# Closing and opening steps of neighbouring attention halves in turn, with values in the keys' PSUM bank

## What is computed

```python
x = x + tanh(g_xattn[l]) * attention_l(layernorm(x), ctx, ...)   # attention half, A
x = x + tanh(g_ffn[l])   * feed_forward_l(layernorm(x), ...)     # feed-forward half, F
# layers 0, 1, 2: 16 heads of width 8 over 77 keys; layer 1 also computes a temperature per head from
# statistics of the scores; layer 3: one softmax over relu projections
# F0: two matmuls around a relu, in 8 chunks of 128 hidden units
# F1: 4 experts of 512, gated (silu(up) * gate), top 2; F2: 8 experts of 352, the same; F3: 8 experts of 128x128
```

## Time and profile before

| | |
|---|---|
| median of 3 runs | 1136.41 us (1135.51 to 1141.63) |
| the profiled execution: device time | 1137.24 us |
| its span (first to last instruction) | 1135.5 us |
| busy: PE, DVE, ACT, POOL | 83%, 63%, 40%, 9% of the span |
| mean granted TensorE clock | 0.912 of full speed |
| loading and turning of weights, before the first unit | about 66 us |
| attention units 0 to 11 | 66 to 891 us |

### The profile page before, as it was taken

One profiled execution on the slowest core, in us unless ns is written; L12 is line 12 of the kernel. 1 busy time (PEld: TensorE's weight loads), 2 busy tenths in 40 slices (PEclk: granted clock), 3 DMA queues, 4 the chain that ended last, 5 costly groups with the idle time before them and its releaser, 6 DMA issues.

```text
span 1135.5 us, 14471 instructions
## 1 busy us (share of the span) xinstructions
PE 944.7 (83%) x4795; PEld 624.7 (55%) x4795; DVE 711.9 (63%) x2190; ACT 459.6 (40%) x1101; POOL 105.9 (9%) x175
## 2 busy tenths in 40 slices
PE   2468899887777886987899899999999888979967
PEld 1434444433333355656567667666767666657744
DVE  0871433517538369579585665776776578887845
ACT  1515345455647645645635316335325222212110
POOL 3100000002103013012000100100100100000000
PEclk8669789999678898998999989999999899999987
DMA  9300000000000000000000000000000000000000
GB/s 262 118 1 1 1 1 1 1 1 1 0 1 1 1 1 1 1 1 1 1 1 2 1 1 1 1 1 1 1 1 1 1 1 10 1 10 1 1 10 9
DMA packets 12065, 12.72 MB, mean 11 GB/s; under 512 B 3758, under 2 KB 7896, under 8 KB 11992
## 3 DMA queue, kind: packets, MB, share of 16 engines
q10 hardware_dynamic: 5536, 8.04, 2.4%
q1 hardware_dynamic: 6072, 3.24, 1.1%
q0 software_dynamic: 384, 0.53, 0.3%
HBM read 10.75 MB, written 1.05 MB: 10 GB/s over the span
## 4 chain that ended last, share of the span: by engine, by line
PE 53%; DVE 28%; ACT 6%; issue 5%; POOL 2%; POOLq 0%; ACTq 0%; DVEq 0%
PE bank L1597 9%; PE bank L1585 5%; PE bank L1507 5%; PE bank L1587 4%; PE bank L1586 4%; PE bank L1392 4%; PE bank L1522 4%; DVE x L1302 3%; DVE hb L1286 3%; DVE nm L1142 3%; DVE hb L1277 3%; DVE x L1266 2%; PE bank L1562 2%; ACT PTs L946 2%; PE bank L1568 2%
## 5 line engine op out<-in xcount | busy, mean ns | idle before, releaser
L983 ACT ACTIVATE hb<-bank 96x512 f32<-96x512 f32 (+1 forms) x160 | 95.5, 597 | 262.6 <-PE bank L1587 261.7
L1585 PE MATMUL bank<-parts,m_w_lo 128*96 128x512 f32 (+1 forms) x320 | 151.0, 472 | 37.0 <-DVE hb L1277 30.0
L1597 PEld LDWEIGHTS bank<-m_w,hb 128*128 128x128 f32 (+1 forms) x1280 | 166.2, 197 | 26.8 <-issue 11.9
L1597 PE MATMUL bank<-m_w,hb 128*128 128x128 f32 (+1 forms) x1280 | 178.8, 284 | 0.5
L1286 DVE SCALAR_TENSOR_TENSOR hb<-hb,bank 96x512 f32<-96x512 f32 (+1 forms) x160 | 108.9, 680 | 87.8 <-ACT hb L983 87.4
L1587 PE MATMUL bank<-parts,m_w_hi 128*96 128x512 f32 (+1 forms) x320 | 128.9, 403 | 0.0
L1586 PE MATMUL bank<-parts,m_w_hi 128*96 128x512 f32 (+1 forms) x320 | 128.7, 402 | 0.0
L1277 DVE TENSOR_TENSOR hb<-hb,bank 96x512 f32<-96x512 f32 (+1 forms) x160 | 109.8, 686 | 11.5 <-PE bank L1587 6.4
L1585 PEld LDWEIGHTS bank<-parts,m_w_lo 128*96 128x96 f32 (+1 forms) x320 | 60.3, 189 | 82.6 <-DVE hb L1277 47.2
L1522 PE MATMUL bank<-Qs,KT 112*77 112x512 f32 x192 | 96.6, 520 | 6.8 <-ACT PTs L946 5.6
L1018 DVE RECIPROCAL rden<-bank 128x16 f32<-128x16 f32 x48 | 12.2, 255 | 130.8 <-PE bank L1345 130.8
(11 more groups left out here) (272 smaller groups left out, 1544.0 us busy)
## 6 DMA issues: line engine op xcount, KB each, us to landing
m_w<-in_L_ffn_w_dram ACTq DMA_DIRECT2D x2, 1024.0 KB, 11.4
nat_m<-in_L_ffn_W_dram ACTq DMA_DIRECT2D x1, 1408.0 KB, 16.7
x<-in_x_dram SPq DMA_DIRECT2D x4, 256.0 KB, 8.1
out_dram<-x SPq DMA_DIRECT2D x4, 256.0 KB, 2.0
f_out<-in_L_ffn_Wout_dram POOLq DMA_DIRECT2D x8, 64.0 KB, 7.9
m_w<-in_L_ffn_W_experts_dram ACTq DMA_DIRECT2D x1, 512.0 KB, 17.1
ctxn<-in_ctx_dram SPq DMA_DIRECT2D x4, 38.5 KB
Wq<-in_L_xattn_Wq_dram SPq DMA_DIRECT2D x2, 64.0 KB
```

What stands on the lines that cost most here:

```text
L983: act.activation(hb[n % 3][0:m, :], bank[UP[u, n]][0:m, :], ACT.Tanh, scale=0.5).then_inc(*chunk_act.up(u, n))
L1585: pe.matmul(dst, w_lo, x_hi, start=True, stop=False)
L1597: op = pe.matmul(bank[7][:, t * P:(t + 1) * P], hb[n % 3][0:m, t * P:(t + 1) * P], wd, start=i == 0 and t == 0, stop=ends_expert(k, n) and ...
```

## The change

It takes turns: after each of the first six closing steps of attention unit i comes one of the first six opening steps of unit i + 1 (`EARLY = 6`). The weights follow: a unit's list loses its own six opening steps (unit 0 keeps them) and gains six at its end, all of weight 0.5. To let both sets of steps be open at once, the banks change: the values go into bank 0 behind the keys' columns, V before K, and ACT copies both only when both are there; the turned x goes into bank 1 in layers 0 to 2, so that bank 2 is free for turning `att`. The first query matmul in bank 0 waits for the values' copy as well.

```diff
@@ -675,6 +675,8 @@
     S1 = S0 + NS
     RING = (1, 0, 2, 3)
     TURN = (4, 5)
+    EARLY = 6
+    XA = {"A3": 2, "F3": 2}
     LATE = 2
 
     def ends_expert(k, n):
@@ -710,7 +712,9 @@
         k = kind(u)
         if k in MHA:
             block, after = (1.8, 0.8) if k == "A1" else (0.5, 0.6)
-            return [1.0] * S0 + [block] * NS + [after] * (steps_pre(k) - S1) + [0.75] * steps_body(k) + [0.6] * steps_tail(k)
+            pre = [1.0] * S0 + [block] * NS + [after] * (steps_pre(k) - S1)
+            tail = [0.6] * steps_tail(k) if u[1] + 1 == ATTENTIONS else [0.5] * (steps_tail(k) + EARLY)
+            return pre[EARLY if u[1] else 0:] + [0.75] * steps_body(k) + tail
         return [1.0] * (steps_pre(k) + steps_body(k))
 
     def steps_f(u):
@@ -761,10 +765,17 @@
 
     def run(pre, body, tail):
 
+
         def attention():
+            ahead = pre(("A", 0))
             for i in range(ATTENTIONS + 2 * STREAMS):
-                u = ("A", i)
-                yield from chain(pre(u), body(u), tail(u))
+                yield from chain(ahead, body(("A", i)))
+                ahead = pre(("A", i + 1))
+                for at, _ in enumerate(tail(("A", i))):
+                    yield
+                    if i + 1 < ATTENTIONS and at < EARLY:
+                        next(ahead)
+                        yield
 
         def feed_forward():
             yield from pre(("F", 0))
@@ -851,7 +862,7 @@
 
                 def normalized():
                     act.wait_ge(*x_turned.at(u, T - 1))
-                    act.activation((xfa if half == "A" else xff[s])[:], bank[2 if half == "A" else UP[u, "x"]][:], ACT.Copy, scale=m2_rms[:, 0:1] if k == "F2" else 1.0) \
+                    act.activation((xfa if half == "A" else xff[s])[:], bank[XA.get(k, 1) if half == "A" else UP[u, "x"]][:], ACT.Copy, scale=m2_rms[:, 0:1] if k == "F2" else 1.0) \
                         .then_inc(*xf_ready.up(u))
 
                 for i in range(steps_pre(k)):
@@ -864,14 +875,14 @@
                             if u[1]:
                                 act.wait_ge(*keys_ready.at(("A", u[1] - 1), J - 1))
                             act.wait_ge(*k_psum.at(u))
+                            act.wait_ge(*v_psum.at(u))
+                            act.activation(VP[:, :, 0:HD],
+                                           bank[0][0:S2, G * S2:G * S2 + P].rearrange("p (h d) -> p h d", d=HD), ACT.Copy,
+                                           scale=mk[b][:, 1:2] if l == 2 else 1.0).then_inc(*values_ready.up(u))
                             for g in range(G):
                                 act.activation(Ksp[:, g, :].bitcast(F32R), bank[0][0:QK, g * S2:(g + 1) * S2], ACT.Identity,
                                                bias=bcol[0:QK, l, 1, g:g + 1],
                                                accum_out=ksum[0:QK, g:g + 1] if l == 1 else None).then_inc(*k_high.up(u, g))
-                            act.wait_ge(*v_psum.at(u))
-                            act.activation(VP[:, :, 0:HD],
-                                           bank[1][0:S2, 0:P].rearrange("p (h d) -> p h d", d=HD), ACT.Copy,
-                                           scale=mk[b][:, 1:2] if l == 2 else 1.0).then_inc(*values_ready.up(u))
                         if i == 4:
                             normalized()
                         if Q0 < i <= Q0 + G:
@@ -1350,7 +1361,7 @@
                 half, s, k, y = u[0], side(u), kind(u), stream(u)
                 l = int(k[1])
 
-                c, xn, xf = (2, xna, xfa) if half == "A" else (UP[u, "x"], xnf, xff[s])
+                c, xn, xf = (XA.get(k, 1), xna, xfa) if half == "A" else (UP[u, "x"], xnf, xff[s])
 
                 def transpose_x():
                     free(c)
@@ -1374,14 +1385,12 @@
                         if i == 2:
                             free(0)
                             pe.wait_ge(*ctx_ready.at(y))
+                            pe.matmul(bank[0][0:S2, G * S2:G * S2 + P], ctxT[y][:], Wv[l][:], start=True, stop=True) \
+                                .then_inc(*v_psum.up(u))
                             for g in range(G):
                                 op = pe.matmul(bank[0][0:QK, g * S2:(g + 1) * S2], WkR[l][:, g, :], ctxT[y][:], start=True, stop=True)
                             op.then_inc(*k_psum.up(u))
                             reader[0] = (k_low, u, G - 1)
-
-                            free(1)
-                            pe.matmul(bank[1][0:S2, 0:P], ctxT[y][:], Wv[l][:], start=True, stop=True).then_inc(*v_psum.up(u))
-                            reader[1] = (values_ready, u)
                         if i == 3:
                             transpose_x()
                         if Q0 <= i < S0:
@@ -1389,6 +1398,8 @@
                             b = RING[g % 4]
                             pe.wait_ge(*xf_ready.at(u))
                             free(b)
+                            if b == 0:
+                                pe.wait_ge(*values_ready.at(u))
                             pe.matmul(bank[b][0:QK, :], WqR[l][:, g, :], xf[:], start=True, stop=True).then_inc(*q_psum.up(u, g))
                             reader[b] = (q_low, u, g)
                         if S0 <= i < S1:
```

## The result

| | before | changed |
|---|---|---|
| median of the runs | 1136.32 us (4 runs, 1135.51 to 1141.63) | 1074.47 us (4 runs, 1072.7 to 1075.48) |
| ratio, 95% interval | | 0.9444, 0.9415 to 0.9474 |
| profiled execution: span, mean granted clock | 1135.5 us, 0.912 | 1073.7 us, 0.934 |

A forecast was written before the change was run, and what follows sets the result against it. It took PE's idle time at the eleven handovers, 37.5 us, as the most that could come back. Terms of 4.9 + 11.8 + 10.5 = 27.2 us off the profiled 1137.24 gave 1110.0, against the median 1109 us, range 1097 to 1124.

The forecast's parts named there:

- Handover 0: Copy to first query: 5.4 us less at full clock, about 4.4 partly at half clock; 4.9 taken.
- The recovered idle time, 27.2 us: Sum over all eleven handovers: 4.9 + 11.8 + 10.5, out of 37.5 us of PE idle time.
- Handovers 6 to 10: Beside F1 and F2: 13.47 us of PE idle time, 0.6 left at each, so 10.5 us gained.
- The banks: Keys and values sharing one bank: at most 0.67 us per handover, covered by the sum and the idle time left.
- gate matmul of handovers 9 and 10: Sign of success: no wait of about 2 us before the first gate matmul there; largest before was 2.13.
- the later addition to x: x is added after the opening's DVE work; its readers have slack; price if not, 2.2 us a handover.
- Rival D: Slower: the opening's 4.1 us on DVE jams its queue and holds gate matmuls; 1154 us, chance 0.04.
- the first step: Handovers 1 to 5: gain counted by PE's idle time, not the chain, since moved work must still be done.
- the rule: Handovers 1 to 5: idle time less 1.5 us each, 19.32 - 5 x 1.5 = 11.8 us.
- the second step: Whole kernel: no gain from TensorE's granted clock counted in the sum beyond handover 0.
- Rival C: The clock gives more: dips at and near handover 0 go, four falls give 12 us; 1097 us, chance 0.09.
- two terms for a fall: Half clock costs 0.7 us on K's matmul and 1.4 on the first three query matmuls, called some 3.

The follow-up runs named there:

- e4: Kernel before, old order and banks, with unread matmuls added in TensorE's waits at handovers 0 to 5: 1130.87 us, ratio 0.9925.
- e3: Changed kernel with turns at handovers 6 to 10 only; 0 to 5 in the order and weights of before, banks as changed: 1129.17 us, ratio 0.9914.
- e1: Kernel before with the bank changes alone, no turns, weights as before: 1140.51 us, ratio 1.0016.
- f1: Kernel before with more unread matmuls in PE's waits at handovers 0 to 5, and also in unit 1: 1132.98 us, ratio 0.9965.
- e6: Changed kernel, turns kept, with the weights of before (closing step 0.6, opening step 1.0): 1085.33 us, ratio 0.953.
- e9: Kernel before with the changed banks and new weights but without the turns: 1129.17 us, ratio 0.9921.
- e12: e6 with three unread matmuls ahead of each of PE's waits for query groups 1, 2 and 3 in unit 9: 1083.78 us, ratio 0.9538.

## Why the prediction missed

*Right.* Handover 0: the chain gave 5.4 us at full clock, and 5.7 came, of which 5.0 is order (e4); I had taken 4.9 for a half clock that didn't occur. The recovered idle time, 27.2 us, and what is left of it, 10.3; that the sum fits to the tenth is luck, since the first term was too high by 1.5 and the last too low by 1.2. Handovers 6 to 10: 10.5 forecast, 11.8 found, 10 by e3. There "what is moved must still be done" holds: the handovers themselves are 24.6 us shorter and the stretches between them 12.8 longer. The banks cost nothing (e1, in the old order). No gate matmul of handovers 9 and 10 waits for DVE any more. No instruction is shown waiting for the later addition to x (110.76 in the timeline). Rival D, DVE's jam, did not come.

*Wrong, the first step: "I count by PE's idle time and not by the chain, since what is moved must still be done".* It holds PE's busy time fixed, and that fell by 31.5 us for the same 4795 matmuls, 26.8 of them up to handover 6. For handovers 1 to 5 the rule gave 11.8 us; handover 2 shows the fault at a clock of 1.00. Handover 2 had 3.79 us of idle time and 6.81 of PE; the rule gives 2.3. It became 4.3 us shorter. Of PE's 6.81 us it now has 5.21. The stretch behind it holds 0.5 us more of PE and yet *fell* by 1.0 in length, because it had 2.6 us of idle time of its own and now has 1.1. Together they are 5.3 us shorter. Of that 4.2 is idle time: the moved work was done in waits that I had not looked at (the earlier trace rows shows 6.4 us of idle time in unit 3, of which I counted only those in the handover). The other 1.1 is busy time, 42.79 us before and 41.70 now for the same 198 matmuls at the same clock; why, no run shows. Over six handovers the full-clock runs (e4, f1) give 5.0 + 5.1 + 4.4 + 3.8 + 5.7 + 7.4 = 31.4 us of order. What is left to the 37 of f1 lies in the stretches, where 1.0 each was seen at full clock in units 2 and 3: 37, against 16.7.

*Wrong, the second step: "I put no clock into the sum beyond handover 0".* The row of handovers 0 to 6 has a clock of 0.87 before and 0.93 now: 98 and 46 us at half clock. At 0.3 us each the 52 us are worth some 16; the pair f1 and changed kernel says 12. Rival C had the right mechanism and 12 us above the sum, with a chance of 0.09. Its size is luck: its two terms for a fall, 0.7 and 1.4, make 2.1 us and not "some 3", so four falls would be 8. Its place was right in half: by the rows, 28 of the 52 us lie in units 1, 4 and 5 and the rest in the handovers. The Trainium skill (TensorE: Matmul & The Clock Gate, HAM oscillation) prices throttled time at half its length; by that, an estimate, the 52 us would be worth 26. The runs show less, 0.3 us per us. That DVE and ACT set part of the pace there is the likely reason, and not a tested one.

*Together:* 37 of order and 12 to 16 of clock in the first six, 12 in the rest, against 61.8 measured. The 12 of clock is what the 37 leave over, so this sum closes by itself; its check from another side is the 16. What stays open is where clock and order part in each unit: executions of the same instructions differ by 4 us in unit 5 and by 6 and 7 after unit 11. That the turns keep the clock up in the handovers is shown by e6 beside e9, not how.

## What to carry to other kernels

PE's idle time at a joint is no ceiling for what overlapping two chains there can bring: price the chain itself, and take the moved work off again only as far as its new neighbourhood has no idle time of its own. On an in-order engine look first for the instruction that stands behind a late one without needing it (here `xna` behind the addition to x). With the statistics alone ahead of it 21 of 62 us came, with the step that holds `xna` 58. And where the granted clock is below 1.00, closing waits of a microsecond can also shorten the busy time around them, so a sum needs a term for it.

## What the runs showed of the hardware

The clock can stay at half while PE has no idle time at all. In e6 a wait of 0.61 us ended 1 us before the fall at 598.0, and a wait of 0.36 us came 1 us after it. Then, with PE busy for 5.00 of 5.00 us and still for 10.00 of 10.00, the clock was 0.50 and, from 620 to 630 us, 0.57; with three unread matmuls at three places around these waits it stayed at 1.00 (e12; one profiled execution of each). The changed kernel has one wait of 1.18 us at the same place of unit 9 and a clock of 1.00 there, so the length of a wait doesn't foretell the fall. A us at half clock cost about 0.3 us over handovers 0 to 6 and 0.35 in unit 9, where PE had almost no idle time.
